# Convolutions on one NeuronCore: the 13x13 convolution in five products a channel, MLP weights loaded in the attention's tail, the fusion bias loaded and centred early

## What is computed

```python
x = attention_in_8x8_windows(x) ; x = x + mlp(layernorm(x))                    # L0, 192 -> 768 -> 192
x = x + gelu(layernorm(fusion_w @ [sobel_x(x), sobel_y(x)] + fusion_b))        # L1
x = x + down(grn(gelu(up(layernorm(dwconv7x7(x))))))                           # L2, 192 -> 768 -> 192
out = bn(dwconv(x, w_lk 13x13)) + sum(bn(dwconv(x, w_i, dilation r_i)))        # L3, per channel
```

## Time and profile before

| | |
|---|---|
| median of 3 runs | 3388.57 us (3385.88 to 3396.99) |
| the profiled execution | 3389.24 us |
| its span | 3387.5 us |
| TensorE matmul busy | 3271.3 us, 97% of the span |
| VectorE, ScalarE, GpSimd busy | 2623.6, 2015.8, 1339.9 us |
| moved by DMA | 555.81 MB, 164 GB/s on average |

### The profile page before, as it was taken

How to read it: one execution, slowest core, us unless ns; L and a number is a source line. 1 busy time by engine, 2 the same in 40 slices (tenths; PEclk the granted TensorE clock), 3 DMA queues, 4 the chain that set the end, 5 groups by cost and what they waited for, 6 DMA issues and landing times. The chain is left out here.

```text
span 3387.5 us, 88476 instructions
## 1 busy us (share of the span) xinstructions
PE 3271.3 (97%) x31488; PEld 3201.6 (95%) x31488; DVE 2623.6 (77%) x6557; ACT 2015.8 (60%) x5417; POOL 1339.9 (40%) x2738
## 2 busy tenths in 40 slices
PE   8999999999799999999969979999999899999999
PEld 6999999999799999999969979989999899999999
DVE  6888888888477777767669989979999788875554
ACT  5778878888344444444437756668999555532222
POOL 5777777777333333333214300024444466630000
PEclk9999999999899999999989989999999999999999
DMA  2444444321144444444369966645555788877775
GB/s 73 130 152 152 156 153 152 122 59 38 27 134 142 133 148 127 137 131 137 115 181 297 284 195 198 198 123 163 170 164 165 222 233 234 236 229 225 228 229 170
DMA packets 473932, 555.81 MB, mean 164 GB/s; under 512 B 79446, under 2 KB 332828, under 8 KB 473500
## 3 DMA queue, kind: packets, MB, share of 16 engines
q1 hardware_dynamic: 445844, 530.67, 53.0%
q10 hardware_dynamic: 27656, 19.48, 1.8%
HBM read 404.55 MB, written 258.73 MB: 196 GB/s over the span
## 5 line engine op out<-in xcount | busy, mean ns | idle before, releaser
L1594 PE MATMUL PS<-dw_grid,dw_mats 128*128 128x196 f32 (+1 forms) x3840 | 627.2, 327 | 26.7 <-DVE dw_mats L1523 26.7
L1594 PEld LDWEIGHTS PS<-dw_grid,dw_mats 128*128 128x128 f32 x3840 | 626.4, 192 | 27.1 <-issue 27.1
L1404 PE MATMUL PS<-mlp_w,mlp_hid 128*128 128x192 f32 x2352 | 414.4, 326 | 0.9 <-ACT mlp_hid L904 0.9
L1519 DVE COPY dw_grid<-X 32x392 f32<-32x392 f32 (+1 forms) x480 | 290.3, 605 | 158.9 <-PE PS L1594 147.9
L1404 PEld LDWEIGHTS PS<-mlp_w,mlp_hid 128*128 128x128 f32 x2352 | 378.6, 190 | 1.2 <-ACT mlp_hid L904 1.2
L1949 PE MATMUL PS<-grn_gain,down_hi 128*128 128x384 f32 x1176 | 352.3, 361 | 10.5 <-POOL X_low L1902 10.5
L1239 POOL TENSOR_TENSOR X<-X,mlp_b 128x192 f32<-128x192 f32 x196 | 112.5, 594 | 542.0 <-DVE mlp_xn L853 536.1
L904 ACT ACTIVATE mlp_hid<-PS,mlp_b 128x256 f32<-128x256 f32 x588 | 246.6, 471 | 111.3 <-PE PS L895 111.2
L610 ACT ACTIVATE att_vbd<-PS,att_rs 64x96 f32<-64x96 f32 x784 | 263.9, 337 | 21.0 <-DVE att_rows L522 13.6
L1902 POOL TENSOR_TENSOR X_low<-X,down_hi 128x128 fp32r<-128x128 f32 x196 | 214.0, 1092 | 146.7 <-ACT down_hi L1912 146.7
L1561 ACT ACTIVATE dw_res<-PS,dw_brow 128x196 f32<-128x196 f32 x192 | 81.5, 424 | 296.8 <-PE PS L1594 296.8
(11 more groups left out here) (283 smaller groups left out, 10197.8 us busy)
## 6 DMA issues: line engine op xcount, KB each, us to landing
scratch_hid<-hid_hid SPq DMA_DIRECT2D x196, 320.0 KB, 3.4
down_hid<-scratch_hid SPq DMA_DIRECT2D x196, 320.0 KB, 3.7
scratch_wide<-scratch_taps SPq DMA_DIRECT2D x64, 960.0 KB, 6.4
dw_raw<-scratch_wide SPq DMA_DIRECT2D x96, 640.0 KB, 4.4
scratch_wide<-scratch_taps SPq DMA_DIRECT2D x64, 768.0 KB, 4.8
dw_raw<-scratch_wide SPq DMA_DIRECT2D x96, 512.0 KB, 3.7
scratch_u<-mlp_u SPq DMA_DIRECT2D x56, 378.0 KB, 3.7
att_x<-in_x SPq DMA_DIRECT2D x196, 96.0 KB, 3.4
```

Of the source, the lines that this page charges most:

```text
L1404: last = nc.tensor.matmul(psD[i], hid[:, p.buf(2), m, i * 128:(i + 1) * 128], w2[:, m, :], start=(m == 0), stop=(m == MC - 1))
L1519: last = nc.vector.tensor_copy(dst, src)
L1594: last = nc.tensor.matmul(dst[:, :, ys, :], m, src, start=(i == 0), stop=(i == len(steps) - 1))
```

## The change

Three parts.

**13x13.** `grid` gets a fifteenth line of zeros, so that the output of a pair of images has 15 lines of patches instead of 14 (`NOUT`, 210 columns). The output patches lie two rows above the input's: patch line b of the output holds the image rows 8b-2 to 8b+5. So it needs its own line of input patches, the line above, and of the line below only the first four rows (32 of 128 pixels), and these only for its last four rows (64 of 128 outputs). The taps of a channel in `raw` have 20 rows as before; the matrices in `mats` take 16 of them, and `top` = 4 go into `corner`. The products are now (own line, h=0) with 210 columns, (own, h=1) with 196, (above, h=0 and h=1) with 196 each, and one with 182 columns for the rest: its matrix is `corner`, 64 outputs wide, and its operand `below` holds the first 32 pixels of each half, once for each of four positions (`h`, `v`), stacked in the partitions. Per pair VectorE copies four corners in addition; ScalarE makes two of the four copies into `below`, GpSimd the other two; TensorE waits for both once a pair, ahead of the first channel's corner product. `out` holds 15 lines of patches, 120 rows an image, and the host part keeps the rows 2 to 113.

**MLP weights.** A new class `FirstWeights` loads fc1's weights, gain, shift and fc2's weights on SP inside `attention`, when its last `half_b` product is done. The fc1 bias has its own semaphore and is loaded at the MLP's start on SP, behind fc2's bias. VectorE splits the weights right after the normalization of the first pair. TensorE does half of the shift products ahead of the first transposes and half behind them.

**Fusion bias.** It is cleared by GpSimd behind its first constants, loaded by ScalarE's queue at the MLP's start, and centred at the middle of the MLP.

```diff
+class FirstWeights:
+    def load(self, sp, a):
+        self.up.load(sp, self.raw, a["L0_conv_fc1_w"])
+        self.up.load_vectors(sp, a["L0_conv_ln2_g"], a["L0_conv_ln2_b"])
+        sp.dma_start(self.w2[:, :, :], a["L0_conv_fc2_w"].rearrange("(m p) n -> p m n", m=MC)).then_inc(self.w2loaded, 16)
...
 def attention(nc, a, d, X, PS, expanded, first_weights, stack):
...
+            sp.wait_ge(q["half_b"], NB)
+            first_weights.load(sp, a)
...
 def mlp_and_sobel(nc, a, d, X, PS, base, expanded, weights):
...
-            w1.load(sp, w1raw, a["L0_conv_fc1_w"])
-            sp.dma_start(w2[:, :, :], ...).then_inc(q["w2loaded"], 16)
-            sp.dma_start(b2[:, :], a["L0_conv_fc2_b"].partition_broadcast(128)).then_inc(q["w2loaded"], 16)
+            sp.dma_start(b2[:, :], a["L0_conv_fc2_b"].partition_broadcast(128)).then_inc(q["b2loaded"], 16)
+            w1.load_bias(sp, a["L0_conv_fc1_b"])
             edges.load_weights(sp)
...
             n.constants(pool)
+            edges.clear_bias(pool)
...
-                        pool.wait_ge(q["w2loaded"], 32)
+                        pool.wait_ge(q["b2loaded"], 16)
...
-                if t.n == NP + 1:
-                    pool.wait_ge(q["biased"], NB)
-                    edges.clear_bias(pool)
...
-            body(Step(0, 0, U))
-            body(Step(0, 1, U))
+            one, two, three = (Step(0, j, U) for j in range(3))
+            for b in one.blocks():
+                n.stats(dve, b)
+            n.normalize(dve, one)
             w1.split(dve, w1raw)
-            body(Step(0, 2, U))
+            for b in two.blocks():
+                n.stats(dve, b)
+            n.low(dve, one)
+            n.normalize(dve, two)
+            for b in three.blocks():
+                n.stats(dve, b)
             w1.bias(dve)
...
                 if j == NP // 2:
                     edges.centre_weights(dve)
+                    edges.centre_bias(dve)
                 if j == NP + 2:
-                    edges.centre_bias(dve)
...
-            w1.load_vectors(act, a["L0_conv_fc1_b"], a["L0_conv_ln2_g"], a["L0_conv_ln2_b"])
+            edges.load_bias(act)
...
-                if t.n == NP + 3:
-                    edges.load_bias(act)
...
+            w1.shift_bias(pe, w1raw, range(MC // 2))
             n.transpose(pe, Step(0, 0, U))
-            w1.shift_bias(pe, w1raw)
+            w1.shift_bias(pe, w1raw, range(MC // 2, MC))
             w1.formed(pe)
...
 def depthwise(...):
-    rows = 24 if tall else 16
+    rows = 16
+    top = NROWS[turn] - rows
...
+    res = s.sb("res", [128, 2, G, NOUT]) if tall else None
+    below = s.sb("below", [128, R, 2, IMG * BY, BX]) if tall else None
+    corner = s.sb("corner", [128, R, 2, top, 16]) if tall else None
...
+    def belows(t, b):
+        pair = bass.ds(t.n * 2, 2)
+        for h in range(2):
+            lines = X[64 * h:64 * h + 32, :, pair].rearrange("p (r x) c -> p c r x", x=BX)
+            for v in range(2):
+                first_x = h + v - 1
+                to = slice(max(0, first_x), BX + min(0, first_x))
+                yield (below[64 * h + 32 * v:64 * h + 32 * v + 32, b.buf(R), :, :, to],
+                       lines[:, :, :, to.start - first_x:to.stop - first_x])
...
+    BELOW_ACT = 2
...
+            def body(t):
+                b = t.ahead(first)
+                pool.wait_ge(q["conv"], b.n * 2 - 2 * R + 2)
+                for at_, src in list(belows(t, b))[BELOW_ACT:]:
+                    last = nc.gpsimd.tensor_copy(at_, src)
+                last.then_inc(below_pool, 1)
...
                 for h in range(2):
-                    last = nc.vector.tensor_copy(mats[:, b.buf(R), :, h, held, :], toeplitz(b, h))
+                    last = nc.vector.tensor_copy(mats[:, b.buf(R), :, h, :, :], toeplitz(b, h))
+                if tall:
+                    for at_, taps in corners(b):
+                        last = nc.vector.tensor_copy(at_, taps)
...
+                if t.inside(CP) and tall:
+                    b = t.ahead(first)
+                    act.wait_ge(q["conv"], b.n * 2 - 2 * R + 2)
+                    for at_, src in list(belows(t, b))[:BELOW_ACT]:
+                        last = nc.scalar.activation(at_, src, ACT.Identity)
+                    last.then_inc(below_act, 1)
...
-                        steps = [(oy, h, 8 * (1 - oy), slice(max(0, -oy), BY - max(0, oy))) for oy in (0, -1, 1) for h in range(2)]
+                        steps = [(0, 0, 0, slice(0, BY + 1)), (0, 1, 0, slice(0, BY)), (-1, 0, 8, slice(1, BY + 1)), (-1, 1, 8, slice(1, BY + 1))]
...
+                        if tall and i == len(steps) - 1:
+                            if c == 0:
+                                pe.wait_ge(below_act, t.n + 1)
+                                pe.wait_ge(below_pool, t.n + 1)
+                            taps = corner[:, b.buf(R), c, :, :].rearrange("p r c -> p (r c)")
+                            src = below[:, b.buf(R), c, :, :].rearrange("p (i y) x -> p i y x", i=IMG)[:, :, 1:BY, :]
+                            nc.tensor.matmul(dst[128 - top * 16:128, :, 0:BY - 1, :], taps, src, start=False, stop=False)
```

More of the change, by code:

```diff
@@ L759, in __init__ @@
         self.gb = s.sb("gb", [128, 2, 2])
-        self.q = {x: s.sem(x) for x in ("loaded", "w1_ready", "shift", "high")}
+        self.q = {x: s.sem(x) for x in ("loaded", "bias_loaded", "w1_ready", "shift", "high")}
     def load(self, eng, raw, w):
@@ L769, in load_vectors, with load_bias, shift_bias @@
                 eng.dma_start(self.gb[at_, i, slot:slot + 1], vector[rows].rearrange("(p o) -> p o", o=1)).then_inc(self.q["loaded"], 16)
[L770 to L775, removed]
+    def load_bias(self, eng, b):
+        eng.dma_start(self.b1[:, :], b.rearrange("(m p) -> p m", m=MC)).then_inc(self.q["bias_loaded"], 16)
+    def shift_bias(self, pe, raw, part=range(MC)):
+        pe.wait_ge(self.q["loaded"], 16 * 3 * len(self.PACKED))
+        for m in part:
             cols = slice(m * 128, (m + 1) * 128)
@@ L778, in shift_bias @@
             last = self.nc.tensor.matmul(self.psB[:, m:m + 1], raw[0:64, 1, cols], self.gb[0:64, 1, 1:2], start=False, stop=True)
-        last.then_inc(self.q["shift"], 1)
+        if MC - 1 in part:
+            last.then_inc(self.q["shift"], 1)
     def formed(self, eng):
@@ L1446, in depthwise @@
     tall = turn == 1
-    rows = 24 if tall else 16
-    held = slice(2, 2 + NROWS[turn]) if tall else slice(0, rows)
+    rows = 16
+    top = NROWS[turn] - rows
     raw = s.sb("raw", [128, R, 2, RUN[turn]])
     mats = s.sb("mats", [128, R, 2, 2, rows, 16])
-    grid = s.sb("grid", [128, R, 2, IMG, BY + 1 - turn, BX + 1])
+    grid = s.sb("grid", [128, R, 2, IMG, BY + 1, BX + 1])
     brow = s.sb("brow", [128, C])
-    res = s.sb("res", [128, 2, G, NB]) if out is not None else None
+    wide_out = NOUT if tall else NB
+    res = s.sb("res", [128, 2, G, NOUT]) if tall else None
+    below = s.sb("below", [128, R, 2, IMG * BY, BX]) if tall else None
+    corner = s.sb("corner", [128, R, 2, top, 16]) if tall else None
+    below_act, below_pool = (s.sem("below_act"), s.sem("below_pool")) if tall else (None, None)
+    clears = 5 if tall else 2
     first = turn * CP
@@ L1458, in ps, with corners @@
     def ps(b, c):
-        return PS[:, 2 * b.buf(4) + c, 0:NB]
+        return PS[:, 2 * b.buf(4) + c, 0:wide_out]
     def toeplitz(b, h):
-        return view(raw[:, b.buf(R), 0, 0:1], [[RUN[turn], 2], [GP, NROWS[turn]], [1, 16]], 16 * h)
+        return view(raw[:, b.buf(R), 0, 0:1], [[RUN[turn], 2], [GP, rows], [1, 16]], GP * top + 16 * h)
+    def corners(b):
+        for h in range(2):
+            for v in range(2):
+                taps = view(raw[64 * h:64 * h + 32, b.buf(R), 0, 0:1], [[RUN[turn], 2], [GP, top], [1, 16]], 16 * v)
+                yield corner[64 * h + 32 * v:64 * h + 32 * v + 32, b.buf(R), :, :, :], taps
+    def belows(t, b):
+        pair = bass.ds(t.n * 2, 2)
+        for h in range(2):
+            lines = X[64 * h:64 * h + 32, :, pair].rearrange("p (r x) c -> p c r x", x=BX)
+            for v in range(2):
+                first_x = h + v - 1
+                to = slice(max(0, first_x), BX + min(0, first_x))
+                yield (below[64 * h + 32 * v:64 * h + 32 * v + 32, b.buf(R), :, :, to],
+                       lines[:, :, :, to.start - first_x:to.stop - first_x])
     def copies(t, b):
@@ L1500, in _ @@
             nc.gpsimd.memset(lines[:, :, 0:BX + 1:BX], 0.0).then_inc(q["cleared"], 1)
[L1501 to L1505, removed]
-                pool.wait_ge(q["cleared"], 1)
-            nc.gpsimd.memset(edges, 0.0).then_inc(q["cleared"], 1)
+            edges = view(grid[:, 0, 0, 0, 0, 0:1], [[(BY + 1) * (BX + 1), 2 * IMG * R], [BY * (BX + 1), 2], [1, BX + 1]])
+            pool.wait_ge(q["cleared"], 2 * turn + 1)
+            nc.gpsimd.memset(edges, 0.0).then_inc(q["cleared"], 1)
+            if not tall:
+                return
```

(8 more changed lines are left out.)

56 lines of the change are left out of this document (32 added, 24 removed).

## The result

| | before | after | ratio (95% interval) |
|---|---|---|---|
| median of 17 runs each | 3393.31 us | 3405.11 us | 1.0034 (1.0024 to 1.0044) |
| the profiled execution | 3389.24 us | 3401.74 us | |
| its span | 3387.5 us | 3399.8 us | |

What follows compares the result with a forecast made beforehand. TensorE alone was taken to bound the 13x13 stage. 3389.2 - 45.5 - 7.0 - 8.1 + 0.8 + 0.2 = 3329.6, on the median's scale 3329 us; bounds of its parts 3322 to 3337, range 3320 to 3384.

Steps and rivals of the forecast that it cites:

- Part 1, TensorE's price: 13x13 stage: five products, 980 columns a channel at 1.694 ns, make a pair 3.32 us; saves 45.5 us.
- the rivals: Grid copies also shutting GpSimd out 0.30, whole records excluding each other 0.08, an unfulfilled stall 0.10, transfers pacing 13x13 0.02.
- Part 1, VectorE and GpSimd: 13x13 stage: only tap and corner copies shut GpSimd out, at most 3.32 us a pair; TensorE stays the bound.
- the first rival: 13x13 stage: grid copies shut GpSimd out too; pair 3.43 to 4.01 us, time 3339 to 3395 us; chance 0.30.
- the upper end of their bounds: 13x13 stage: GpSimd's two copies take 0.99 to 1.58 us a pair; the upper, 850 and 730 ns, was taken.
- the signs of being wrong: 13x13 stage: GpSimd copies over 1.2 us, or grid/tap copies over 607/424 ns, and TensorE waiting for VectorE or GpSimd each pair.
- The stage's start: Before the first 13x13 matmul: four corner copies, 0.89 us, less 0.13 us for smaller tap copies; +0.8 us.
- Part 2: MLP's start: weights loaded in the attention's tail bring the second pair's transposes 7.0 us earlier, bounds 4 to 8.
- what the bounds had named: MLP's start: saving only 4 us if the weight split and GpSimd's additions shut each other out.
- Part 3: Passage from MLP to Sobel: early fusion bias removes VectorE's wait, saving 8.1 us, from below 5.
- late next: MLP to Sobel: last strip load, 7.7 us from its issue, arrives at 1709.0; VectorE wants it at about 1709.
- DMA: 13x13 stage: taps and output need 262 GB/s, which fits; the rival that it paces the stage had chance 0.02.

Runs made afterwards that it cites:

- the padded kernels: Changed kernel, corner matrix zero-padded to 128 columns: 3395.15 us; also GpSimd's copies left out: 3334.54; or all `below` copies by ScalarE from `grid`: 3333.96.
- the runs with one edit: Changed kernel with GpSimd's copies left out after the first four pairs: 3401.13 us; changed kernel with corner matrix zero-padded to 128 columns: 3395.15 us.
- the last version: Changed kernel with corner matrix zero-padded to 128 columns and all four `below` copies made by ScalarE out of `grid`: 3333.96 us, ratio 0.9829 to before.

## Why the prediction was wrong, point by point

**Part 1, TensorE's price: wrong.** The step that failed is "a product is paid by its columns, so I count it in full". Columns were indeed paid at 1.694 ns, but the change to the narrow operand and back came on top, 0.34 us a channel, 65 us. In the 13x13 stage of before no row could show it, since all its products had one width. The rest of that trace has narrow operands, and they speak against the width alone as the cause. TensorE's transposes of L0 and L2 (line 866) have operands of 128 and 64 columns in turn and write to PSUM partitions from 0 up. First the group of narrow loads in L2, then a timeline in L0:

```profile
L866 PEld LDWEIGHTS PS<-hid_ident,hid_xn 128*64 128x64 f32 x196 | 22.0, 112 | 0.0
```

```profile
1206.46 0.60 PE L866 MATMUL PS<-mlp_ident,mlp_xn 128*128 128x128 f32 x4
1206.89 0.65 PE L1404 MATMUL PS<-mlp_w,mlp_hid 128*128 128x192 f32 x3
```

The narrow loads wait for nothing, where the corner's 384 loads wait 45.0 us, and four transposes of 128 columns, two of them with a narrow operand, take 0.43 us: 0.85 ns a column, half of 1.694 for one instruction instead of two.

What the corner product has besides its width is an output in the upper 64 partitions (64 to 127), and it is a product, not a transpose. Which of the two makes the price is open; the padded kernels took away the width and the place together. A rule was at hand, and I did not weigh it: the Trainium skill (TensorEngine Tiling (Array Packing), section Key Properties) says that a change of the tiling mode drains the engine. No view here shows the engine's mode; if the corner product is such a change, the traces agree and give the price, for which the page has none. None of the rivals had this mechanism.

**Part 1, VectorE and GpSimd: wrong in the forecast, right in the first rival.** The forecast held that 0.85 + 0.89 + 1.58 = 3.32 us "is the most that excludes each other in a pair". Two things fail there. The sum leaves VectorE's own 1.21 us of grid copies out, which hide nothing of GpSimd's work unless that falls on them; it falls where TensorE's `conv` releases it, 0.1 us before the grid copies end (3103.22 above). And judging by rate, I took the grid copies for harmless; where GpSimd met them they took 976 ns in the mean. The first rival had both, and at its upper bound 4.01 us a pair; VectorE needs 4.00. Its range ended at 3395 us, its chance was 0.30. GpSimd's copies stood at the upper end of their bounds, 850 and 730 ns: the shortest took 0.82 and 0.73 us. Their means, 861 and 852 ns, hold waiting too. Two rows, the first copy of each engine in the pair shown above, tell how they exclude each other:

```profile
3103.22 0.85 POOL L1563 COPY dw_below<-X 32x392 f32<-32x392 f32 x1 [2.25 <-PE PS L1668]
3103.36 1.00 DVE L1581 COPY dw_mats<-dw_raw 128x512 f32<-128x512 f32 x1
```

The tap copy ends 0.29 us after GpSimd's. Alone it takes 0.42, so 0.13 us of it were hidden, as the prediction had it from the earlier trace rows. The Trainium skill's rule (SBUF — State Buffer, section Who interferes with whom), that the one that starts first holds the shared ports for the whole instruction, agrees but for these 0.13 us with the tap copies at 968 ns and the grid copies at 976; rows of the MLP had made me doubt it. The judgement by rate was weak besides: 768 elements in 0.61 us, read as two per 1.04 ns, are 0.79 ns an element with the fixed cost in it. Of the signs of being wrong that the prediction named, the longer tap copies came; TensorE waited for neither engine, since it had a bound of its own.

That both bounds stand within 0.1 us of each other is chance: one comes from the gaps at the switches, the other from the copies. It hid each of them behind the other, and the runs with one edit told them apart.

**The stage's start: mis-sized.** I counted +0.8 us for four corner copies. TensorE's wait grew from 6.06 to 10.08 us, 4.0 us. GpSimd's first eight copies, all released at once, run 7.6 us beside VectorE's, so the first two tap copies take 1.62 us in place of 0.85, and the four corner copies 3.30 in place of 0.90. First the row of before, then those after:

```profile
3016.15 1.32 PE L1594 MATMUL PS<-dw_grid,dw_mats 128*128 128x196 f32 x3 [6.06 <-DVE dw_mats L1523]
```

```profile
3000.91 7.63 POOL L1563 COPY dw_below<-X 32x392 f32<-32x392 f32 x8
3003.00 1.62 DVE L1581 COPY dw_mats<-dw_raw 128x512 f32<-128x512 f32 x2 [0.24 <-DMA dw_raw<-scratch_wide]
3004.54 3.30 DVE L1584 COPY dw_corner<-dw_raw 32x128 f32<-32x128 f32 x4
...
3007.95 2.35 PE L1668 MATMUL PS<-dw_grid,dw_mats 128*128 128x210 f32 x6 [10.08 <-DVE dw_corner L1584]
```

The stage thus runs 387.2 us from the first product to the last (3007.95 to 3395.15) against 367.3 in the earlier trace rows, +19.9; with +4.0 at its start +23.9.

**Part 2: right in its mechanism, 1 us too large.** The attention's last product before, and the timeline of the MLP's start after:

```profile
863.54 0.41 PE L692 MATMUL PS<-att_wpr,att_ol 97*128 97x192 f32 x1
```

```profile
864.84 0.41 PE L711 MATMUL PS<-att_wpr,att_ol 97*128 97x192 f32 x1
...
871.24 0.83 POOL L1260 TENSOR_TENSOR X<-X,mlp_b 128x192 f32<-128x192 f32 x1 [0.26 <-DVE mlp_xn L876]
871.54 0.94 DVE L269 TENSOR_SCALAR mlp_wb_hi<-mlp_w1raw,mlp_gb 128x768 fp32r<-128x768 f32 x1
...
877.65 1.08 PE L889 MATMUL PS<-mlp_ident,mlp_xn 128*128 128x128 f32 x4 [2.61 <-DVE mlp_xn L876]
```

The second transposes start at 877.65 instead of 882.40, 4.75 us earlier, though the attention ended 1.3 us later (865.25 against 863.95). That is 6.05 us against 7.0. A third of the difference is what the bounds had named: the second multiply of the split takes 0.94 us instead of 0.61, beside GpSimd's addition. Most of the rest is the normalization of the second pair, 1.23 us (from 876.32) where before it took 0.66; it too runs beside GpSimd's work. The attention's later end is no cost that the runs show: in the seven traces with the changed attention it comes between 861.79 and 868.64, and the 863.95 of before lies among them. From there to the second transposes they all take 12.4 to 12.5 us, against 18.45 before.

**Part 3: right, its last tenth by chance.** The first Sobel product starts at 1705.44 instead of 1718.32, 12.9 us earlier; less the 4.75 us from the MLP's start that is 8.1, as forecast (7.5 to 8.2 in the seven traces that have the change). Before and after:

```profile
1718.32 1.97 PE L1158 MATMUL PS<-sobel_wf,sobel_edge 128*128 128x192 f32 x5 [0.79 <-DVE sobel_edge L1078]
```

```profile
1705.44 4.85 PE L1181 MATMUL PS<-sobel_wf,sobel_edge 128*128 128x192 f32 x14 [2.27 <-DVE sobel_edge L1101]
```

Waits of VectorE from 1690 to 1716 us (in total, times, longest); there are four, the longest 0.9 us, and none is for the bias:

```profile
DVE X L1343 <- PE PS L1428: 1.3, 2, 0.8
...
DVE sobel_edge L1097 <- DMA sobel_xu<-scratch_u: 0.8, 1, 0.8
DVE sobel_edge L1097 <- DMA sobel_xm<-scratch_w: 0.4, 1, 0.4
```

A strip load is late next, though not the one that was named: ahead of the first Sobel product VectorE waits 0.35 us for `sobel_xm`, and 0.47 for TensorE. The forecast had left out that the centring, 0.93 us before (1708.34 to 1709.27), leaves this place as well; the two new waits take nearly as much.

**DMA: right.** At 3.32 us a pair it moves 264 GB/s without holding anything up.

**The sum.** 3401.74 in the profile against 3329.6: 65 us for the changes to the corner product and back (or, if these were gone, nearly as much for VectorE and GpSimd), 3 us at the stage's start, 1 us in part 2, 1.3 us of a later attention, the rest below a microsecond each. Without both bounds the forecast of part 1 stands: in the last version the 13x13 stage, from the end of the stage ahead of it to its last product, is 45.4 us shorter than before, where 44.7 were forecast (45.5 less 0.8 at the start), and the time is 3334 us. Two slips of the prediction changed nothing: the two stores of the earlier trace rows go to different slots of `res`, with two pairs between them all the same, and the bounds of its parts don't give the 3322 us at the lower end.

## What to carry to other kernels

A smaller stationary operand saves nothing by its width, and a 64-column product into the upper partitions between 128-column ones costs 0.34 us here: pad it with zeros, or put two in a row. Work for an idle GpSimd is not free while VectorE copies fp32 inside SBUF; add both engines' times unless a row shows that they overlap, and look for what releases each of them. VectorE's other copies need their time as well. Where two engines are both busy without a wait, there may be two bounds: take away each alone and both together before calling one the cause.

## What the runs showed of the hardware that was not expected

- A change from 128-column products to a 64-column one with its output in partitions 64 to 127, and back, costs TensorE 0.34 us, with one such product between or with two (4.00 us a pair with four changes of width, 3.65 with two, 3.31 with none). The width alone is free in the transposes of L0 and L2, which write to partitions from 0 up (0.0 us of waiting ahead of the 196 narrow loads of L2). A 64-column product into the lower partitions was not tried.
- VectorE's strided fp32 copy at 1.55 ns an element and GpSimd's copies exclude each other as the fast ones do: 976 ns in place of 608. At a change from one engine to the other 0.13 us overlap.
- ScalarE reads 364 elements in runs of 7 in 502 ns, 392 strided ones in 884.
